# The last expert layer in 39 slots of 128 rows with copied input weights, and eight weight chunks split during the first routing

## The chip, the cores and the metric

One core of one Trainium2 chip. The metric is the device time of one execution in microseconds (us). The engines are TensorE (PE, its weight loads PEld), VectorE (DVE), ScalarE (ACT), GpSimd (POOL) and SyncE (SP, which only issues DMAs here). They run their own instruction streams and meet at semaphores.

## The reference

Two layers on x of 2 x 1024 tokens of width 256. Each adds an attention-like part and then a mixture of 8 experts of which each token uses 2. Only the expert parts matter here:

```python
x = x + _L0_xattn_ref(_layernorm(x), ctx, ...)      # attention to 77 context rows
x = x + _L0_ffn_ref(_layernorm(x), ...)             # experts 256 -> 256 -> 256
x = x + _L1_xattn_ref(_layernorm(x), ctx, ...)      # a linear map
x = x + _L1_ffn_ref(_layernorm(x), ...)             # experts 256 -> 1024 -> 256
# _L1_ffn_ref
probs = softmax(x @ router_w.T + router_b); top_p, top_e = top_k(probs, 2)
for e in range(8):
    y = y + gate_e[:, None] * (gelu(x @ w1[e].T + b1[e]) @ w2[e].T + b2[e])
```

## The kernel before

All matrix products that matter are done in three fp16 products: each fp32 operand is kept as a high part and a low part (the rest), and `three` (line 1204, whose `mm` is line 1202) adds high x high, high x low and low x high in PSUM.

**Order of the stages.** Attention over 16 tiles of 128 tokens; routing of the first expert layer (`route(0)`); its slots; a token stage that gathers the expert results, adds the linear map and normalizes; routing of the last expert layer (`route(1)`); its slots; the sum into the output.

**Routing.** `route` on DVE is a chain of some fifty small operations on 128 x 128 numbers (lines 979 to 1060), with two products on TensorE between and one multiplication on POOL (`number_tokens`, line 527). It sorts the 4096 (token, expert) pairs by expert, each expert padded up to whole slots, and ends with `index`, the token of each place, from which POOL gathers. ACT adds two exponentials, which DVE waits for behind `index`.

**Slots.** A slot is 256 rows (`A = 2` tiles of 128) of one expert. Their number is fixed at the worst case, `NSLOT = (2*T + E*(SW-1)) // SW` = 23, 5888 rows. For slot j: POOL gathers two tiles of normalized rows from DRAM (`gather_rows`, line 536, two slots ahead, three buffers); TensorE transposes them (`slot_tr`, line 1400); DVE copies the columns out of PSUM (`slot_cols`, line 1068); TensorE multiplies by the expert's input weights (`slot_up`); DVE scales and adds the bias (`slot_bias`, line 1081); ACT applies gelu and writes the high part (lines 737, 741); DVE writes the low part (`slot_lo`, line 1090); TensorE multiplies by the output weights (`slot_down`); DVE adds the output bias (`slot_out`, line 1099). In the first layer SP stores the result, in the last one POOL scatters it by token (`scatter_y`, line 578). In the last layer a slot has 48 up matmuls whose stationary operand is a weight tile and whose moving operand is 256 rows, and 48 down matmuls whose moving operand is 256 weight columns. The expert of a slot is read into a register, and weights and biases are addressed through it:

```python
last = three(ps[:, hc, :], m.wa[:, bass.ds(e + o, P)], m.wa[:, bass.ds(e + (per + o), P)],
             xT[:, dc, :], xT[:, DC + dc, :], dc == 0, dc == DC - 1)
```

**Weight chunks.** The expert weights come as 44 chunks, most of 128 x 1024 fp32 (512 KB). SP loads a chunk into a staging buffer (`stage`); ACT writes the high part (`split_hi`, line 608), and for the chunks whose low part POOL makes also scales the staged values (line 611); the low part is made by POOL (`split_lo`, line 452, even chunks) or by DVE (line 849, odd chunks). Chunks 4 to 19 are split during attention, 20 to 39 one per slot step of the first expert layer, and the last four (40 to 43, all by POOL) just before POOL's part of the second routing. Four staging buffers are in turn from chunk 22 to 37.

**Queues.** Each engine works strictly in the order of its code. In the first layer POOL's order is: gather of slot j+2, then the low part of chunk 20+j if it is even. SP's order is: chunk 24+j, then the store of slot j-4; the bias broadcast `b2_loaded0` (1 MB) goes out once `index` is there. In the last layer POOL's is: gather of slot j+2, scatter of slot j-3.

## Time and profile before

| | |
|---|---|
| median of 3 runs | 822.01 us (821.63 to 823.38) |
| profiled execution | 821.37 us, its span 819.5 us |
| TensorE busy | 610.7 us, 75% of the span |
| DVE busy | 544.0 us, 66% |
| ACT busy | 378.6 us, 46% |
| POOL busy | 434.1 us, 53% |
| TensorE clock granted, mean | 0.872 of full speed |
| DMA | 70.27 MB, 86 GB/s over the span |

The span is the time from the first to the last instruction of the profiled execution; the execution's own time is 1.9 us longer. Busy shares are means over stages that have different limits. Clock 1.00 is 2.4 GHz, 0.50 is 1.2 GHz.

### The profile page before, as it was taken

To read this page: it belongs to the slowest core of one execution; us is meant where nothing else is said; L and a number is where in the kernel's file an instruction comes from. 1 tells how busy PE (TensorE), PEld (TensorE's weight loads), DVE (VectorE), ACT (ScalarE), POOL (GpSimd) and SP (SyncE) were. 2 spreads that over 40 slices of the span, in tenths; PEclk is the share of its full clock that TensorE was granted. 3 is DMA by queue.
4 is the path that set the end of the run, shared out by engine and by line. 5 is a ranking of instruction groups with operands and counts; after the bars stand their busy time and mean duration, and the time that the engine had idled before them with its cause. 6 is when DMAs were issued, how large, how long until landed. Compare 5 with 4: busy or idle time off the path is not lost.

```text
span 819.5 us, 16876 instructions
## 1 busy us (share of the span) xinstructions
PE 610.7 (75%) x5984; PEld 539.1 (66%) x5984; DVE 544.0 (66%) x975; ACT 378.6 (46%) x568; POOL 434.1 (53%) x406
## 2 busy tenths in 40 slices
PE   5957889999996416779544553079999999999960
PEld 4646888889985315567432443068898889888850
DVE  3963689999988675668446776945555555555527
ACT  2644267777765315555314666324344443333420
POOL 6663668988886137767328863453333333332120
PEclk9986699999998757889985776579999999999995
DMA  8201002211222426776742322021111111111018
GB/s 277 78 3 28 26 2 66 66 50 50 66 66 65 118 72 180 220 217 166 219 137 82 98 78 79 5 78 42 50 46 48 53 53 54 48 47 39 21 38 303
DMA packets 35824, 70.27 MB, mean 86 GB/s; under 512 B 5985, under 2 KB 22114, under 8 KB 35490
## 3 DMA queue, kind: packets, MB, share of 16 engines
q1 hardware_dynamic: 25442, 42.70, 16.8%
q0 software_dynamic: 8160, 22.29, 9.8%
q10 hardware_dynamic: 2144, 4.19, 1.4%
q8 instruction: 54, 0.88, 0.5%
q14 instruction: 24, 0.20, 0.1%
HBM read 50.81 MB, written 18.35 MB: 84 GB/s over the span
## 4 chain that ended last, share of the span: by engine, by line
PE 48%; DVE 21%; issue 8%; POOL 8%; DMA 7%; ACT 7%; SPq 0%; POOLq 0%; ACTq 0%; DVEq 0%
PE banks L1202 45%; DMA slot_region<-normed_rows,index 4%; PE banks L1400 2%; POOL wb_region L568 2%; POOL slot_region L536 1%; DVE x_res L1129 1%; DVE w_region L895 1%; DVE rs L887 1%; DVE w_region L900 1%; ACT w_region L675 1%; POOL w_region L452 1%; DMA w_region<-token_y 1%; DVE w_region L1034 1%; DVE slot_region L1034 1%; POOL rv L476 1%
## 5 line engine op out<-in xcount | busy, mean ns | idle before, releaser
L1202 PE MATMUL banks<-w_region 128*128 128x128 f16 (+5 forms) x1948 | 174.9, 251 | 31.9 <-POOL w_region L527 12.1
L1202 PEld LDWEIGHTS banks<-w_region 128*128 128x128 f16 (+1 forms) x1948 | 160.7, 126 | 41.4 <-POOL w_region L527 12.4
L1202 PE MATMUL banks<-w_region,wb_region 128*128 (+1 forms) x1168 | 137.9, 277 | 11.8 <-DMA wb_region<-wk 6.6
L1202 PEld LDWEIGHTS banks<-w_region,wb_region 128*128 128x128 f16 (+1 forms) x1168 | 119.2, 105 | 26.0 <-issue 7.9
L578 POOL DMA_INDIRECT token_y<-slot_region,lg x46 | 45.4, 987 | 157.6 <-DVE slot_region L1099 150.6
L737 ACT ACTIVATE wb_region<-wb_region 128x1024 f32<-128x1024 f32 x46 | 48.6, 1057 | 166.7 <-DVE wb_region L1081 166.7
L1202 PE MATMUL banks<-slot_region,w_region 128*128 128x256 f16 x1104 | 125.3, 274 | 0.0
L1202 PEld LDWEIGHTS banks<-slot_region,w_region 128*128 x1104 | 107.6, 98 | 12.6
L536 POOL DMA_INDIRECT slot_region<-normed_rows,index x92 | 91.9, 999 | 36.2 <-issue 23.8
L1081 DVE SCALAR_TENSOR_TENSOR wb_region<-banks,b_s 128x1024 f32<-128x1024 f32 x46 | 56.2, 1224 | 70.0 <-PE banks L1202 70.0
L1090 DVE TENSOR_TENSOR wb_region<-wb_region 128x1024 f16<-128x1024 f32 x46 | 56.2, 1221 | 25.7 <-ACT wb_region L741 25.7
L1202 PE MATMUL banks<-wb_region,w_region 128*128 (+1 forms) x344 | 54.4, 309 | 16.0 <-ACT w_region L642 10.1
L1202 PEld LDWEIGHTS banks<-wb_region,w_region 128*128 128x128 f16 (+1 forms) x344 | 40.1, 122 | 27.9 <-ACT w_region L642 13.1
L1400 PE MATMUL banks<-ident_h,slot_region 128*128 128x128 f16 x368 | 31.3, 234 | 34.7 <-DMA slot_region<-normed_rows,index 34.5
L487 POOL TENSOR_TENSOR rq<-rq,neghalf 128x16 f32<-128x16 f32 x16 | 47.8, 2984 | 6.8 <-DVE rq L863 6.8
L1400 PEld LDWEIGHTS banks<-ident_h,slot_region 128*128 128x128 f16 x368 | 25.7, 104 | 38.6 <-DMA slot_region<-normed_rows,index 37.2
L741 ACT ACTIVATE wb_region<-wb_region 128x1024 f16<-128x1024 f32 x46 | 48.6, 1057 | 1.5
L1068 DVE COPY slot_region<-banks 128x1024 f16<-128x1024 f16 x46 | 31.4, 683 | 26.7 <-PE banks L1400 26.7
L499 POOL TENSOR_TENSOR w_region<-w_region,rs 128x1232 f32<-128x1232 f32 x16 | 36.0, 2249 | 18.5 <-DVE rs L890 18.4
L452 POOL TENSOR_TENSOR w_region<-staging,w_region 128x1024 f16<-128x1024 f32 x15 | 32.0, 2136 | 22.7 <-ACT staging L611 22.6
L1202 PE MATMUL banks<-slot_region,wb_region 128*128 128x256 f16 x276 | 40.4, 305 | 0.0
L687 ACT ACTIVATE w_region<-banks 128x512 f16<-128x512 f32 (+1 forms) x48 | 23.4, 522 | 36.4 <-PE banks L1313 36.4
(237 smaller groups left out, 1077.2 us busy)
## 6 DMA issues: line engine op xcount, KB each, us to landing
staging<-w_t SPq DMA_DIRECT2D x24, 512.0 KB, 4.2
sorted_y<-slot_region SPq DMA_DIRECT2D x23, 256.0 KB, 4.7
w_region<-w_t SPq DMA_DIRECT2D x8, 512.0 KB, 5.5
x_res<-x SPq DMA_DIRECT2D x4, 512.0 KB, 9.7
staging<-w_in SPq DMA_DIRECT2D x4, 512.0 KB, 3.7
normed_rows<-w_region SPq DMA_DIRECT2D x16, 128.0 KB, 1.7
staging<-w_out SPq DMA_DIRECT2D x4, 512.0 KB, 3.7
normed_rows<-wb_region SPq DMA_DIRECT2D x16, 128.0 KB, 2.0
```

The lines of the kernel that those rows point to most:

```text
L452: g.tensor_tensor(chunks[k][2], staged(k), chunks[k][1], ALU.subtract).then_inc(sem(f"chunk_lo{k % 2}"), 1)
L487: link(g.tensor_tensor(v, v, neghalf[:, 0:1].to_broadcast([P, NH]), ALU.pow))
L499: g.tensor_tensor(p_rows(i), p_rows(i), rs[:, :, None].to_broadcast([P, NH, L]), ALU.mult).then_inc(sem("weights_ready"), 1)
L536: g.indirect_dma_start(out=m.rows[:, j % RING, a, :], out_offset=None, in_=rows_dram, in_offset=bass.IndirectOffsetOnAxis(ap=index[:, q:q ...
L578: g.indirect_dma_start(out=y_token, out_offset=bass.IndirectOffsetOnAxis(ap=back[:, q:q + 1], axis=0), in_=moes[1].y[:, j % YB, a, :], in_ ...
L737: s_.activation(v, v, ACT.Gelu_apprx_tanh).then_inc(sem("gelu"), 1)
L741: s_.activation(m.hh[:, j % 2, a * m.HH:(a + 1) * m.HH, :], v, ACT.Copy).then_inc(sem(f"h_hi{layer}"), 1)
L1068: v.tensor_copy(m.xT[:, j % 2], slot_columns(j)).then_inc(sem(f"slot_cols{layer}"), 1)
L1081: v.scalar_tensor_tensor(out=m.g[:, u % 2], in0=hidden(m, u), scalar=1.0 / WS, in1=bias[:, :, None].to_broadcast([P, m.HH, SW]), op0=ALU.m ...
L1090: v.tensor_tensor(m.hl[:, j % 2, c, :], m.g[:, u % 2], m.hh[:, j % 2, c, :], ALU.subtract).then_inc(sem(f"h_lo{layer}"), 1)
L1202: return t.matmul(o, a, b, start=start, stop=stop)
L1400: last = t.transpose(cols[:, c, a * P:(a + 1) * P], m.rows[:, j % RING, a, c * P:(c + 1) * P], ident_h[:, :])
```

## The change

**Last layer.** Slots are 128 rows (`TILES = (2, 1)`), and there are 39 of them, 4992 rows. The first layer keeps 23 slots of 256. A slot has 4 transposes, 48 up matmuls with 128 moving columns and 24 down matmuls with 256. Gathers run four slots ahead in a ring of eight tiles; results have four buffers. Before each slot DVE copies the high and low input weights of its expert (8 KB a partition) into `w_slot`, which lies over the two staging buffers, in two halves of hidden units (`slot_weights`, each a COPY of 4 x 512 fp16 a partition). The copy of a half waits until TensorE has finished that half of the slot before (`half_up`), and the up matmuls wait for their half's copy and take their weights from the fixed place. Bias, gelu and low part work on the whole slot of 128 x 1024 at once. The last layer's `slot_down` trails `slot_up` by two slots and not by one.

**First routing.** Chunks 20 to 27 (`ROUTED`) are split between attention and slots: ACT makes both of its passes over each of them before `route(0)`'s exponentials, POOL makes all eight low parts before `number_tokens`. SP no longer waits for `index` with the bias broadcast, which goes out behind chunk 23, and then stages up to chunk 31.

**First layer's slots.** Twelve chunks (28 to 39) remain, one at every second slot step, six on POOL and six on DVE. The order of the chunks in memory is changed with that: both weights of experts 0 to 3 first, then those of 4 to 6, then those of 7.

Some semaphores are shared between the layers, with counts that run on.

```diff
-    A = 2
-    SW = A * P
-    NSLOT = (2 * T + E * (SW - 1)) // SW
-    NQ = A * NSLOT
+    TILES = (2, 1)
+    NSLOTS = [(2 * T + E * (a * P - 1)) // (a * P) for a in TILES]
+    NQS = [a * n for a, n in zip(TILES, NSLOTS)]
+    LAG = 2
...
-        chunks += [c for e, c in big if e < E - 1] + [c for e, c in big if e == E - 1]
+
+        for part in (range(E // 2), range(E // 2, E - 1), range(E - 1, E)):
+            chunks += [c for e, c in big if e in part]
...
+        R_CH = 8
         LATE = 2 * (per // CH)
+        ROUTED = range(PRE + A_CH, PRE + A_CH + R_CH)
+        WITH_SLOTS = range(ROUTED.stop, NCH - LATE)
+
+        def by_pool(k):
+            return k % 2 == 0 or k in ROUTED or k >= NCH - LATE
...
-            return k // 2 + 1 if k < NCH - LATE else (NCH - LATE) // 2 + k - (NCH - LATE) + 1
+            return sum(by_pool(n) for n in range(k + 1))
+
+        def chunk_of(s):
+            return WITH_SLOTS[s // 2] if s % 2 == 0 and s // 2 < len(WITH_SLOTS) else None
...
+            m.A, m.NSLOT, m.NQ = TILES[layer], NSLOTS[layer], NQS[layer]
+            m.SW = m.A * P
+            m.RING, m.AHEAD, m.YB = ((3, 2, 3), (8, 4, 4))[layer]
+            m.rows, at = carve(SLR, 0, [m.RING, m.A, 2 * D], F16)
+            m.xT, at = carve(SLR, at, [2, 2 * DC, m.SW], F16)
+            m.y, at = carve(SLR, at, [m.YB, m.A, D], F32)
...
+        w_slot = STG[:, :, :].rearrange("p a b -> p (a b)").bitcast(F16).rearrange("p (s n) -> p s n", n=H1)
...
             for k in RINGED[0:2]:
                 stage(k)
-            sp.wait_ge(sem("routed"), 1)
             load(moes[0].b2, b_out0.partition_broadcast(P), "b2_loaded0")
-            for j in range(NSLOT + 4):
-                if RINGED.start + 2 + j < RINGED.stop:
-                    stage(RINGED.start + 2 + j)
-                elif 0 <= j - len(RINGED) < 4:
-                    stage(RINGED.stop + j - len(RINGED))
+            for k in range(RINGED.start + 2, ROUTED.stop + 4):
+                stage(k)
+
+            stage_at = {k: 2 * (k - 4 - ROUTED.stop) for k in range(ROUTED.stop + 4, RINGED.stop)}
+            stage_at |= {k: 2 * (min(k, RINGED.stop + 1) - 2 - ROUTED.stop) for k in range(RINGED.stop, RINGED.stop + 2)}
+            stage_at[RINGED.stop] = stage_at[RINGED.stop + 1]
+            stage_at |= {k: 2 * (k - 2 - ROUTED.stop) for k in range(NCH - LATE, NCH - LATE + 2)}
+            for j in range(NSLOTS[0] + 4):
+                for k in sorted(stage_at):
+                    if stage_at[k] == j:
+                        stage(k)
                 if j >= 4:
-                    keep_y(0, j - 4)
+                    keep_y(j - 4)
...
             def split_lo(k):
 
                 pool.wait_ge(sem("chunk_scaled"), scaled(k))
+                if k % 2:
+                    pool.wait_ge(sem("chunk_lo1"), k // 2)
                 g.tensor_tensor(chunks[k][2], staged(k), chunks[k][1], ALU.subtract).then_inc(sem(f"chunk_lo{k % 2}"), 1)
...
+                for j in range(m.AHEAD):
                     gather_rows(layer, j)
                 if layer == 1:
                     pool.wait_ge(sem("back_ready"), 1)
-                for j in range(NSLOT + 3 * layer):
-                    if j + AHEAD < NSLOT:
-                        gather_rows(layer, j + AHEAD)
+                for j in range(m.NSLOT + 3 * layer):
+                    if j + m.AHEAD < m.NSLOT:
+                        gather_rows(layer, j + m.AHEAD)
                     if layer == 1 and j >= 3:
                         scatter_y(j - 3)
                     if layer == 0:
-                        k = PRE + A_CH + j
-                        if k < NCH - LATE and k % 2 == 0:
+                        k = chunk_of(j)
+                        if k is not None and by_pool(k):
                             split_lo(k)
...
+            for k in ROUTED:
+                split_lo(k)
             slot_rows(0)
...
+            act.wait_ge(sem("attn_done"), NT)
+            for k in ROUTED:
+                split_hi(k)
             route(0)
             act.wait_ge(sem("gates_ready"), 1)
-            for s in range(NSLOT + 1):
-                if s < NSLOT and PRE + A_CH + s < NCH - LATE:
-                    split_hi(PRE + A_CH + s)
+            for s in range(NSLOTS[0] + 1):
+                if chunk_of(s) is not None:
+                    split_hi(chunk_of(s))
                 if s >= 1:
                     gelu(0, s - 1)
...
+            def expert_at(j):
+                expert_of[j] = dve.value_load(expert[0:1, 0, j:j + 1], min_val=0, max_val=E - 1)
+
+            def slot_weights(j, a):
+
+                m = moes[1]
+                if j >= 1:
+                    dve.wait_ge(sem("half_up"), 2 * (j - 1) + a + 1)
+                half = slice(a * m.H // 2, (a + 1) * m.H // 2)
+                src = m.wa[:, bass.ds(expert_of[j] * (2 * DC * m.H), 2 * DC * m.H)].rearrange("p (s n) -> p s n", n=m.H)
+                v.tensor_copy(w_slot[:, :, half], src[:, :, half]).then_inc(sem("slot_weights"), 1)
+
+            def slot_bias(layer, j):
 
                 m = moes[layer]
-                u = m.PARTS * j + a
-                if a == 0:
-                    expert_of[j] = dve.value_load(expert[0:1, 0, j:j + 1], min_val=0, max_val=E - 1)
-                dve.wait_ge(sem(f"slot_h{layer}"), u + 1)
-                if u >= 2:
-                    dve.wait_ge(sem(f"h_lo{layer}"), u - 1)
-                bias = m.b[:, bass.ds(expert_of[j] * m.HC + a * m.HH, m.HH)]
-                v.scalar_tensor_tensor(out=m.g[:, u % 2], in0=hidden(m, u), scalar=1.0 / WS,
-                                       in1=bias[:, :, None].to_broadcast([P, m.HH, SW]),
-                                       op0=ALU.mult, op1=ALU.add).then_inc(sem(f"h_biased{layer}"), 1)
-
-            def slot_lo(layer, j, a):
+                dve.wait_ge(*up_done(layer, j + 1))
+                if j >= 2:
+                    dve.wait_ge(sem("h_lo"), made(layer, j - 1))
+                bias = m.b[:, bass.ds(expert_of[j] * m.HC, m.HC)]
+                v.scalar_tensor_tensor(out=m.g[:, j % 2], in0=hidden(m, j), scalar=1.0 / WS,
+                                       in1=bias[:, :, None].to_broadcast([P, m.HC, m.SW]),
+                                       op0=ALU.mult, op1=ALU.add).then_inc(sem("h_biased"), 1)
...
+            def slots_of_last():
+                dve.wait_ge(sem("b1_loaded"), 16)
+                dve.wait_ge(sem("b2_loaded1"), 16)
+                for b in range(2):
+                    dve.wait_ge(sem(f"chunk_lo{b}"), NCH // 2)
+                n = NSLOTS[1]
+                for s in range(-1, n + LAG + 1):
+                    if s + 1 < n:
+                        slot_cols(1, s + 1)
+                        expert_at(s + 1)
+                        for a in range(2):
+                            slot_weights(s + 1, a)
+                    if 0 <= s < n:
+                        slot_bias(1, s)
+                    if 0 <= s - LAG - 1 < n:
+                        slot_out(1, s - LAG - 1)
+                    if 0 <= s - 1 < n:
+                        slot_lo(1, s - 1)
...
+            def slot_up_last(j):
+
+                m = moes[1]
+                pe.wait_ge(sem("slot_cols"), made(1, j + 1))
+                if j >= 2:
+                    pe.wait_ge(sem("h_biased"), made(1, j - 1))
+                xT, ps = m.xT[:, j % 2], hidden(m, j)
+                for a in range(2):
+                    pe.wait_ge(sem("slot_weights"), 2 * j + a + 1)
+                    for hc in range(a * m.HC // 2, (a + 1) * m.HC // 2):
+                        w = slice(hc * P, (hc + 1) * P)
+                        for dc in range(DC):
+                            last = three(ps[:, hc, :], w_slot[:, dc, w], w_slot[:, DC + dc, w],
+                                         xT[:, dc, :], xT[:, DC + dc, :], dc == 0, dc == DC - 1)
+                    last.then_inc(sem("half_up"), 1)
```

## Rows read from the trace of the kernel before

**Rows 1.** Windows: start:end, length, busy us (x instructions) by engine, PEclk, DMA share, GB/s.
```profile
270.00:304.00 34.00, 9.17 (x109) 7.50 (x107) 25.92 (x64) 8.32 (x15) 8.38 (x6) 0.63 0.26 78
304.00:425.00 121.00, 83.81 (x736) 68.23 (x736) 71.36 (x105) 59.56 (x77) 69.82 (x58) 0.88 0.67 192
...
536.00:789.00 253.00, 250.06 (x2362) 224.21 (x2363) 139.52 (x137) 97.17 (x92) 85.08 (x87) 0.99 0.16 47
```

**Rows 2.** Timeline of one slot, last layer: start, duration, engine, line, operation [idle before].
```profile
611.50 0.61 PE L1400 MATMUL banks<-ident_h,slot_region 128*128 128x128 f16 x8
...
611.95 5.40 PE L1202 MATMUL banks<-slot_region,w_region 128*128 128x256 f16 x48
...
614.87 1.23 DVE L1081 SCALAR_TENSOR_TENSOR wb_region<-banks,b_s 128x1024 f32<-128x1024 f32 x1 [1.76 <-PE banks L1202]
...
617.19 5.40 PE L1202 MATMUL banks<-w_region,wb_region 128*128 x48
...
622.43 0.61 PE L1400 MATMUL banks<-ident_h,slot_region 128*128 128x128 f16 x8
```

**Rows 3.** Timeline of TensorE in the attention stage.
```profile
130.71 6.12 PE L1202 MATMUL banks<-w_region 128*128 128x128 f16 x78
136.67 1.04 PE L1313 MATMUL banks<-w_region 128*128 128x128 f32 x8
```

**Rows 4.** Groups by line and shape: count, busy us, mean ns, idle before.
```profile
L1202 PEld LDWEIGHTS banks<-slot_region,w_region 128*128 x1104 | 107.6, 98 | 12.6
...
L1090 DVE TENSOR_TENSOR wb_region<-wb_region 128x1024 f16<-128x1024 f32 x46 | 56.2, 1221 | 25.7 <-ACT wb_region L741 25.7
...
L1068 DVE COPY slot_region<-banks 128x1024 f16<-128x1024 f16 x46 | 31.4, 683 | 26.7 <-PE banks L1400 26.7
...
L905 DVE SCALAR_TENSOR_TENSOR x_res<-banks,x_res 128x256 f32<-128x256 f32 x16 | 6.7, 417 | 2.7 <-PE banks L1202 2.6
```

**Rows 5.** Timeline at both ends of the last expert layer.
```profile
532.25 1.07 POOL L536 DMA_INDIRECT slot_region<-normed_rows,index  x1 [4.15 <-DVE index L1049]
...
536.48 1.03 PE L1400 MATMUL banks<-ident_h,slot_region 128*128 128x128 f16 x8 [5.38 <-DMA slot_region<-normed_rows,index]
...
539.71 1.70 PE L1202 MATMUL banks<-slot_region,w_region 128*128 128x256 f16 x7
...
787.13 5.40 PE L1202 MATMUL banks<-w_region,wb_region 128*128 x48 [1.09 <-DVE slot_region L1099]
...
794.94 0.97 POOL L578 DMA_INDIRECT token_y<-slot_region,lg  x1 [0.30 <-issue]
```

**Rows 6.** Timeline: start of the first routing, and its first gather.
```profile
282.87 0.29 DVE L979 TENSOR_REDUCE w_region<-lg 128x16 f32<-128x128 f32 x1
...
304.22 1.23 POOL L536 DMA_INDIRECT slot_region<-normed_rows,index  x1 [4.17 <-DVE index L1049]
```

**Rows 7.** Timeline of the second routing, DVE and POOL.
```profile
505.30 4.25 POOL L452 TENSOR_TENSOR w_region<-staging,w_region 128x1024 f16<-128x1024 f32 x2 [5.05 <-ACT staging L611]
505.42 2.15 DVE L986 SCALAR_TENSOR_TENSOR slot_region<-slot_region,lg 128x128 f32<-128x128 f32 x1
...
507.92 1.77 DVE L981 TENSOR_TENSOR slot_region<-slot_region 128x128 f32<-128x128 f32 x1
509.73 0.29 DVE L982 TENSOR_TENSOR slot_region<-slot_region,first 128x128 f32<-128x128 f32 x1
...
513.34 2.12 POOL L452 TENSOR_TENSOR w_region<-staging,w_region 128x1024 f16<-128x1024 f32 x1 [3.80 <-ACT staging L611]
513.42 2.07 DVE L1001 TENSOR_TENSOR slot_region<-slot_region 128x8 f32<-128x8 f32 x1
```

**Rows 8.** Timeline: TensorE's slot transposes in the first expert layer.
```profile
309.60 1.04 PE L1400 MATMUL banks<-ident_h,slot_region 128*128 128x128 f16 x8 [6.55 <-DMA slot_region<-normed_rows,index]
...
357.63 0.61 PE L1400 MATMUL banks<-ident_h,slot_region 128*128 128x128 f16 x8
...
360.70 0.61 PE L1400 MATMUL banks<-ident_h,slot_region 128*128 128x128 f16 x8
...
409.73 0.61 PE L1400 MATMUL banks<-ident_h,slot_region 128*128 128x128 f16 x8
```

**Rows 9.** Waits, 304 to 425 us: total us, times, longest.
```profile
PE banks L1400 <- DMA slot_region<-normed_rows,index: 27.8, 8, 6.6
```

More of the change, by code:

```diff
@@ L85, in build @@
     VW_STEP = 4
-    AHEAD = 2
-    RING = 3
-    YB = 3
     with ExitStack() as ctx:
@@ L290, in build, with slot_columns, slot_banks, hidden @@
         LAST = slice(FULL * 6, NH)
-        def slot_columns(j):
-            return bank[7 * (j % 2)].bitcast(F16)[:, 0:2 * DC * SW].rearrange("p (c t) -> p c t", t=SW)
-        def slot_banks(j):
-            b = 5 if A == 2 else 5 + j % 2
-            return PSUM[:, b:b + A, 0:D]
-        def hidden(m, u):
-            b = 1 + 2 * (u % 2)
-            return PSUM[:, b:b + 2, :].rearrange("p b (c t) -> p (b c) t", t=SW)[:, 0:m.HH, :]
+        def slot_columns(m, j):
+            return bank[7 * (j % 2)].bitcast(F16)[:, 0:2 * DC * m.SW].rearrange("p (c t) -> p c t", t=m.SW)
+        def slot_banks(m, j):
+            b = 5 if m.A == 2 else 5 + j % 2
+            return PSUM[:, b:b + m.A, 0:D]
+        def hidden(m, j):
+            b = 1 + 2 * (j % 2)
+            return PSUM[:, b:b + 2, :].rearrange("p b (c t) -> p (b c) t", t=m.SW)[:, 0:m.HC, :]
+        def made(layer, n):
+            return layer * NSLOTS[0] + n
+        def up_done(layer, n):
+            return (sem("half_up"), 2 * n) if layer else (sem("slot_h"), n)
+        def gathered(layer, j):
+            k = j % moes[layer].RING
+            first = TILES[0] * len(range(k, NSLOTS[0], moes[0].RING)) if layer and k < moes[0].RING else 0
+            return sem(f"rows_gathered{k}"), 16 * (first + TILES[layer] * (j // moes[layer].RING + 1))
         block = ctx.enter_context(nc.Block())
@@ L531, in gather_rows @@
                 m = moes[layer]
-                for a in range(A):
-                    if j >= RING:
-                        pool.wait_ge(sem(f"slot_tr{layer}"), j - RING + 1)
-                    q = A * j + a
+                for a in range(m.A):
+                    if j >= m.RING:
+                        pool.wait_ge(sem("slot_tr"), made(layer, j - m.RING + 1))
+                    q = m.A * j + a
                     g.indirect_dma_start(
-                        out=m.rows[:, j % RING, a, :], out_offset=None, in_=rows_dram,
+                        out=m.rows[:, j % m.RING, a, :], out_offset=None, in_=rows_dram,
                         in_offset=bass.IndirectOffsetOnAxis(ap=index[:, q:q + 1], axis=0)).then_inc(
-                        sem(f"rows_gathered{layer}_{j % RING}"), 16)
+                        gathered(layer, j)[0], 16)
             def slot_rows(layer):
@@ L545, in slot_rows @@
                     pool.wait_ge(sem(f"rows_kept{1 + 2 * layer}_{b}"), 16 * (NT // 2))
-                for j in range(AHEAD):
+                m = moes[layer]
+                for j in range(m.AHEAD):
                     gather_rows(layer, j)
@@ L1393, in slot_tr @@
                 m = moes[layer]
-                pe.wait_ge(sem(f"rows_gathered{layer}_{j % RING}"), 16 * A * (j // RING + 1))
+                pe.wait_ge(*gathered(layer, j))
                 if j >= 2:
-                    pe.wait_ge(sem(f"slot_cols{layer}"), j - 1)
-                cols = slot_columns(j)
-                for a in range(A):
+                    pe.wait_ge(sem("slot_cols"), made(layer, j - 1))
+                cols = slot_columns(m, j)
+                for a in range(m.A):
                     for c in range(2 * DC):
-                        last = t.transpose(cols[:, c, a * P:(a + 1) * P], m.rows[:, j % RING, a, c * P:(c + 1) * P],
+                        last = t.transpose(cols[:, c, a * P:(a + 1) * P], m.rows[:, j % m.RING, a, c * P:(c + 1) * P],
```

228 lines of the change are left out of this document (110 added, 118 removed).

## The prediction

> **What bounds the kernel now.** I read the page first for its totals, then the busy times by stretch [rows 1]. They show stages with different limits, so the page's 75% busy TensorE says little. In the last expert layer (536 to 789 us) TensorE is busy 250.06 of 253 us at a granted clock of 0.99: nothing else matters there. In the first expert layer (304 to 425) it is busy 83.8 of 121 us, with the DMA engines at 0.67. Between and behind them lie the token stages and the second routing, which the change hardly touches.
>
> Next the timeline of one slot of the last layer [rows 2]. A slot of 256 rows takes 622.43 - 611.50 = 10.93 us. The 48 matmuls of `slot_up` take 617.19 - 611.95 = 5.24 us, 109.2 ns each at 256 columns; `slot_down` is as long; what is left for the 8 transposes is 0.45 us, 56 ns each. So 23 slots are 251 us of pure matmul stream, and the only way to shorten it is to stream fewer columns. For the price of 128 columns I looked for a stretch of the attention stage with such matmuls [rows 3]: 78 matmuls of the `q_proj` and `attn` loops (48 of 128 columns, 30 of 256) run from 130.71 to the next group at 136.67, 5.96 us. Less 30 x 109.2 = 3.28, 48 took 2.68 us, 56 ns each.
>
> **Last layer, the slot.** A slot of 128 rows has 4 transposes (0.22), 48 up matmuls of 128 columns (2.68) and 24 down matmuls of 256 columns (2.62): 5.52 us. 39 of them are 215.3 us, against 251.4. The saving is 4992 padded rows for 5888.
>
> It holds only if DVE keeps up, since it now copies each slot's input weights too: two COPYs of 128x2048 f16 within SBUF. No row has that shape. DVE's rows [rows 4] go from 417 ns at 256 fp32 elements to 1221 at 1024: 1.05 ns an element and 0.15 us fixed. The f16 COPY out of PSUM, 683 ns for 1024, is (683 - 150)/1024 = 0.52 ns an element. At that pace a copy is 0.15 + 1.07 = 1.22 us; the upper end is 0.15 + 2048 x 1.05 = 2.30 us, the lower end the fixed 0.15. I take 1.22, as COPY in f16 is the nearest row. A 512-element column copy is then 0.42, the output add of 256 elements 0.42.
>
> Now the order on DVE. Call T the end of the first half of up(s) on TensorE. DVE sees a finished half 0.30 us later (611.95 + 2.62 = 614.57; the bias starts at 614.87 [rows 2]), and I let following operations overlap by 0.08, as they do in a busy stretch. Copy one runs T+0.30 to 1.44. Copy two waits for the second half (T+1.34+0.30) and ends at 2.78, bias (1.22) at 3.92, output add at 4.26, low part (1.22) at 5.40, columns at 5.74. The next half is due at T+5.52+0.30 = 5.82. So DVE fits with 0.08 us to spare at 1.22 us a copy, and with about 0.6 at half that. Above 1.31 us a copy the slot becomes 2 x copy + 2.9. The read of the expert number in front of the copies I cost at nothing, as a wait stands behind it; without that cover 0.1 us would cost 39 x 0.1 = 4 us. ACT is busy 97 of 253 us with the same passes over 5888 rows [rows 1] and gets fewer; POOL has one gather and one scatter a slot at 0.97 + 0.30 = 1.27 each [rows 5]. Both are hidden under 5.5.
>
> **Last layer, its ends** [rows 5]. The first slot now needs one gather, not two. The first gather is issued at 532.25, and tr(0) now waits until 536.48 for the second one, 1.3 later. tr(0) can come at about 535.1; tr(1) waits for the next gather (536.5), then up(0) starts at about 537.0 and not 539.71: -2.7. The stream from there: 39 x (2.68 + 2.62) + 37 x 0.22 = 214.8, plus 2 for the half clock at its start and 0.4 for the first low part, 217.2. It was 252.7, from 539.71 to 787.13 + 48 x 0.109 = 792.4: -35.5. At the end one scatter of 1.27 and 0.27 of output add go. Together **-39.7 us**. The route arithmetic is as long as before: 39 for 46 columns of places, 273 for 161 expert comparisons, some tenths of either sign.
>
> **First routing.** Before, DVE starts it at 282.87 and the first gather goes out at 304.22 [rows 6], with POOL busy for 8.4 us and ACT for 8.3 of the 34 around it [rows 1]. Now ACT does two passes and POOL one subtraction for each of eight chunks in it, and SP sends the chunks and the bias broadcast (1 MB) earlier. What that costs can be read in the second routing, where POOL splits four late chunks [rows 7]: L986 takes 2.15 us and L981 1.77 while POOL's subtraction runs, against 0.29 for the like operation at 509.73, and L1001 takes 2.07. A DVE operation with two SBUF inputs waits for POOL's subtraction to end. The four stretch by 1.86, 1.48, 1.90 and 1.90: 1.79 on the mean. Eight subtractions, nearly back to back like the first two there (4.25 us for both), each catch one: 8 x 1.79 = **+14.3 us** of later first gather. Bounds: nothing, if all fell into DVE's waits; 8 x 2.13 = 17, and some us more if the chunks come late. POOL's own next work, `number_tokens`, waits for DVE anyway, and ACT's two exponentials are due later than its last chunk.
>
> **First expert layer.** The transposes of its 23 slots start at 309.60 and 409.73 at the ends [rows 8]: 4.55 us a slot. Undisturbed ones follow at 357.63 and 360.70, 3.07 us. The excess is 100.1 - 22 x 3.07 = 32.6 us, of which TensorE waited 27.8 us in 8 waits for gathered rows [rows 9]. These come late because POOL issues them behind a subtraction that waits for ACT and for a chunk, and because 0.5 MB chunks share the DMA engines. Now 12 chunks are split here, not 20, and they are loaded well ahead. If the excess falls with the chunks (12/20), 13 us go; POOL's own demand, 2 x 1.27 + 2.13 x 6/23 = 3.1 a slot, is as long as TensorE's 3.07, so not all 32.6 can go. I take between 13 and 21: **-17 us**. The first gathers also lose the 1 MB broadcast beside them: -1.
>
> **Sum.** -39.7 + 14.3 - 17 - 1 = -43.4. The profiled execution took 821.4 us (span 819.5 and 1.9 around it), which lies 0.6 under the median of 822.0. 821.4 - 43.4 = 778.0.
>
> **Rivals.**
> A, the routing is not stretched, since the chunks come late or fall into DVE's gaps: 778 - 14 = 764. For it: ACT must wait for chunks 22 to 24 through the DMA. Against: later subtractions only meet later DVE operations.
> B, the first layer keeps its pace, bound by the way issue to landing with a ring of three: 778 + 17 = 795. For it: the gathers' waits [rows 9]; against: 3.07 us stretches exist with all chunk work in them.
> C, the weight copies are slow, and DVE bounds the last layer. At one element per 1.05 ns a copy is 2.30, the slot 2 x 2.30 + 2.9 = 7.5: 39 x 2.0 = 78 more, 856 and slower than before. It decides from 1.31 us a copy, and eats the whole gain from 1.88 us. For it: no row has an SBUF copy of this size; against: the pace of the f16 COPY [rows 4].
> D, the weight loads no longer hide. A load lasts 98 ns [rows 4], longer than 56; were it the pace, 48 x 42 = 2.0 us a slot, 39 x 2.0 = 79, 857. Against it are the 48 matmuls of that stretch [rows 3], each with a load of its own. The Trainium skill (TensorE: Matmul & The Clock Gate, section Back-to-back issue gap) says that a stream of load and matmul pairs of 128 columns sustains about 81 ns each. By that figure the slot would grow by 1.2 us and the gain of the last layer would be gone; the 56 ns of this trace disagree.
>
> **How the numbers follow.** Forecast 0.63, A 0.12, B 0.13, C 0.06, D 0.03, others 0.03. The likeliest gives 778, its own range 768 to 789. 762 to 797 takes in A and B and leaves out about 0.15. A difference of 0.2% (1.6 us) is about what can be told from none here. Slower: C, D and a part of the others, 0.09; the same 0.01; faster 0.90.
>
> **What would show it.** Last layer: transposes 5.5 us apart, TensorE without a gap, DVE waiting shortly before each first copy, a COPY of 128x2048 at 1.2 us or less. Routing: two-input DVE operations of about 2 us beside POOL's L452, and the first gather some 35 us after the routing's start instead of 21. First layer: fewer waits for gathered rows, under 4 us a slot. I am wrong if the copy is over 1.3 us, or is itself held by POOL's gathers and scatters, which no row shows.

## The result, and the profile after

The changed kernel took 781.6 us (median of 4 runs, 778.7 to 784.9) where the kernel before took 822.1 us (821.6 to 823.4) beside it. The ratio is 0.9511, with a 95% interval of 0.9477 to 0.9545. The forecast was 778.0, with a range of 762 to 797. A second set of five runs beside eleven of the kernel before, on another chip, gave 782.1 us and a ratio of 0.9534 (0.9511 to 0.9557). The profiled execution of the changed kernel took 783.2 us, with a span of 781.4.

First the granted clock and the busy times by stretch, in the changed kernel: the first expert layer (317 to 426 us) and the last one (538 to 756). Columns as in [rows 1].

```profile
317.00:426.00 109.00, 81.33 (x736) 68.72 (x736) 66.87 (x102) 47.64 (x65) 58.65 (x53) 0.88 0.57 162
538.00:756.00 218.00, 217.39 (x2956) 205.91 (x2954) 166.68 (x231) 82.48 (x78) 107.08 (x73) 0.99 0.15 46
```

TensorE is still full in the last layer, 217.4 of 218 us, and the layer is now 38 us shorter. VectorE (DVE) has gone up there from 139.5 of 253 us [rows 1] to 166.7 of 218.

Next the timeline of one slot of the last layer, which answers to [rows 2].

```profile
639.89 0.39 PE L1464 MATMUL banks<-ident_h,slot_region 128*128 128x128 f16 x4
...
640.12 2.84 PE L1265 MATMUL banks<-slot_region,staging 128*128 128x128 f16 x48
...
641.77 0.69 DVE L1119 COPY staging<-w_region 128x2048 f16 x1 [0.56 <-PE banks L1265]
642.04 1.26 POOL L570 DMA_INDIRECT slot_region<-normed_rows,index  x1 [0.30 <-issue]
...
642.80 2.78 PE L1265 MATMUL banks<-w_region,wb_region 128*128 x24
643.11 0.70 DVE L1119 COPY staging<-w_region 128x2048 f16 x1 [0.65 <-PE banks L1265]
643.73 1.21 DVE L1128 SCALAR_TENSOR_TENSOR wb_region<-banks,b_s 128x1024 f32<-128x1024 f32 x1
644.86 0.41 DVE L1143 SCALAR_TENSOR_TENSOR slot_region<-banks,wb_region 128x256 f32<-128x256 f32 x1
...
645.19 1.21 DVE L1135 TENSOR_TENSOR wb_region<-wb_region 128x1024 f16<-128x1024 f32 x1
...
645.42 0.39 PE L1464 MATMUL banks<-ident_h,slot_region 128*128 128x128 f16 x4
```

The slot takes 645.42 - 639.89 = 5.53 us, forecast 5.52. The 48 up matmuls go from 640.12 to the down products at 642.80, 2.68 us, 56 ns each, as priced from [rows 3]. DVE's order is the one of the prediction, and it waits 0.56 and 0.65 us before the two copies. Each copy takes 0.70 us, not 1.22.

Then the first routing, where the second group answers to [rows 6] and the first to what was expected from [rows 7]: DVE and POOL, timeline.

```profile
283.08 0.29 DVE L1018 TENSOR_REDUCE w_region<-lg 128x16 f32<-128x128 f32 x1
...
284.58 2.12 POOL L485 TENSOR_TENSOR w_region<-staging,w_region 128x1024 f16<-128x1024 f32 x1 [5.15 <-ACT staging L647]
284.70 2.15 DVE L1025 SCALAR_TENSOR_TENSOR w_region<-w_region,lg 128x128 f32<-128x128 f32 x1
...
291.33 4.30 POOL L485 TENSOR_TENSOR w_region<-w_region 128x1024 f16<-128x1024 f32 x2
291.79 1.79 DVE L1039 COPY w_region<-w_region 128x7 f32<-128x7 f32 x1
293.62 2.04 DVE L1040 TENSOR_TENSOR w_region<-w_region 128x8 f32<-128x8 f32 x1
...
317.44 1.24 POOL L570 DMA_INDIRECT slot_region<-normed_rows,index  x1 [4.17 <-DVE index L1088]
```

From the routing's start to the first gather it is now 34.36 us; it was 21.35. Each of POOL's eight subtractions holds one DVE operation until it ends: a copy of 7 elements lasts 1.79 us, and 0.17 in the kernel before. The eight held operations together last 13.0 us longer than the same operations in the kernel before, which is the whole delay.

Last, the slot transposes of the first layer and TensorE's waits for gathered rows in it, which answer to [rows 8, 9].

```profile
321.75 1.03 PE L1464 MATMUL banks<-ident_h,slot_region 128*128 128x128 f16 x8 [5.47 <-DMA slot_region<-normed_rows,index]
...
410.11 0.61 PE L1464 MATMUL banks<-ident_h,slot_region 128*128 128x128 f16 x8
```

```profile
PE banks L1464 <- DMA slot_region<-normed_rows,index: 21.5, 8, 5.5
```

22 steps take 88.4 us, 4.02 us a slot; it was 4.55 [rows 8]. The waits went only from 27.8 to 21.5 us, still eight of them. The first of them (6.6 us before, 5.5 now) stands ahead of the first transposes and so outside these 22 steps.

The two profiled executions differ by 819.5 - 781.4 = 38.1 us, which splits at four landmarks (after minus before). Start of routing to first gather: +13.0. First gather to the end of the first layer (POOL's iota, which waits for the last kept rows, 425.84 against 424.14): -11.5. From there to the first gather of the last layer (532.31 against 532.25): -1.6. From that gather to the last scatter: -38.1. What lies ahead of the routing and behind the last scatter makes up the rest, +0.1.

### The profile page after: what moved, and what is told of

The parts are those of the page before. It is cut to its first block, busy times and chain, and to the rows that moved or that the text cites. A ratio compares the mean times of both kernels' runs of the same rounds, so it can differ in the third digit from the quotient of the medians.

```text
span 781.4 us, 17877 instructions
## 1 busy us (share of the span) xinstructions
PE 574.4 (74%) x6556; PEld 520.0 (67%) x6556; DVE 578.9 (74%) x1067; ACT 368.2 (47%) x558; POOL 461.5 (59%) x396
## 4 chain that ended last, share of the span: by engine, by line
PE 46%; DVE 25%; issue 8%; ACT 7%; POOL 7%; DMA 6%; SPq 0%; DVEq 0%; ACTq 0%; POOLq 0%
PE banks L1265 43%; DMA slot_region<-normed_rows,index 4%; PE banks L1464 2%; POOL wb_region L603 2%; DVE x_res L1191 1%; DVE w_region L933 1%; DVE heads L925 1%; DVE w_region L938 1%; ACT w_region L711 1%; POOL slot_region L570 1%; DMA w_region<-token_y 1%; DVE w_region L1073 1%; DVE slot_region L1073 1%; DVE w_region L861 1%; ACT w_region L687 1%
## 5 line engine op out<-in xcount | busy, mean ns | idle before, releaser
L1265 PE MATMUL banks<-w_region,wb_region 128*128 (+1 forms) x1000 | 122.2, 278 | 11.3 <-DMA wb_region<-wk 6.9
L612 POOL DMA_INDIRECT token_y<-slot_region,lg x39 | 65.6, 1682 | 101.5 <-DVE slot_region L1143 101.2
L1265 PEld LDWEIGHTS banks<-w_region,wb_region 128*128 128x128 f16 (+1 forms) x1000 | 101.4, 107 | 22.8 <-issue 8.0
L1265 PE MATMUL banks<-slot_region,staging 128*128 128x128 f16 x1872 | 112.9, 221 | 0.7 <-DVE staging L1119 0.7
L1265 PEld LDWEIGHTS banks<-slot_region,staging 128*128 128x128 f16 x1872 | 108.1, 99 | 1.0 <-issue 0.9
L1119 DVE COPY staging<-w_region 128x2048 f16 x78 | 54.4, 700 | 46.2 <-PE banks L1265 45.7
L520 POOL TENSOR_TENSOR heads<-heads,neghalf 128x16 f32<-128x16 f32 x16 | 47.7, 2982 | 6.8 <-DVE heads L901 6.8
L1128 DVE SCALAR_TENSOR_TENSOR wb_region<-banks,b_s 128x1024 f32<-128x1024 f32 x39 | 47.1, 1207 | 2.0 <-PE banks L1265 2.0
L532 POOL TENSOR_TENSOR w_region<-w_region,heads 128x1232 f32<-128x1232 f32 x16 | 36.0, 2248 | 18.5 <-DVE heads L928 18.4
L1107 DVE COPY slot_region<-banks 128x512 f16<-128x512 f16 (+1 forms) x62 | 31.7, 511 | 14.7 <-PE banks L1464 14.6
```

What stands on the lines that cost most here:

```text
L520: link(g.tensor_tensor(v, v, neghalf[:, 0:1].to_broadcast([P, NH]), ALU.pow))
L532: g.tensor_tensor(p_rows(i), p_rows(i), rs[:, :, None].to_broadcast([P, NH, L]), ALU.mult).then_inc(sem("weights_ready"), 1)
L612: g.indirect_dma_start(out=y_token, out_offset=bass.IndirectOffsetOnAxis(ap=back[:, j:j + 1], axis=0), in_=m.y[:, j % m.YB, 0, :], in_offs ...
L1119: v.tensor_copy(w_slot[:, :, half], src[:, :, half]).then_inc(sem("slot_weights"), 1)
L1128: v.scalar_tensor_tensor(out=m.g[:, j % 2], in0=hidden(m, j), scalar=1.0 / WS, in1=bias[:, :, None].to_broadcast([P, m.HC, m.SW]), op0=ALU ...
L1265: return t.matmul(o, a, b, start=start, stop=stop)
```

## The experiments

The 12 kernels ran in three groups of four; each was timed beside the kernel before on its own chip, so ratios are compared, not times. The kernel before stood at 826.9, 819.9 and 819.4 us in the three.

### The two parts alone

The last layer alone: the changed kernel, with

```
-        R_CH = 8
+        R_CH = 0
-            return WITH_SLOTS[s // 2] if s % 2 == 0 and s // 2 < len(WITH_SLOTS) else None
+            return WITH_SLOTS[s] if s < len(WITH_SLOTS) else None
```

and SyncE's order of loads as in the kernel before. The new order of the chunks in memory stays.

> The last layer as after the change, the weight chunks split where the kernel before splits them (none in the first routing, one with each slot of the first layer). Theory: the whole gain is the last layer's (the traces give it 38.1 us of 38.1), and the chunk part is worth nothing: 13.2 us of later first gather against 12.6 us from the first slots. That gives 783 to 785. Rival, the prediction's own sum (the chunk part is worth -3.7 us): 785 to 787, with the changed kernel at 781.6. Rival two, the chunk part costs something, since its first gathers are later: 778 or less.

Measured: ratio 0.9494 (0.9462 to 0.9526), on the 822 us of the first set 780.5. That is under the 783 to 785 expected, and its interval (777.9 to 783.1) leaves out the 785 to 787 of the prediction's sum. The last layer alone gives as much as both parts, as far as these intervals can tell.

The chunks alone: the kernel before with

```
+        R_CH = 8
+            for k in ROUTED:
+                split_lo(k)
             slot_rows(0)
...
+            act.wait_ge(sem("attn_done"), NT)
+            for k in ROUTED:
+                split_hi(k)
             route(0)
```

and `chunk_of`, `by_pool`, SyncE's order and the order of the chunks in memory of the changed kernel.

> The kernel before, with the changed kernel's schedule of weight chunks and nothing else. Theory: about 822 as before, within 2 us, as 13.2 us of later first gather are given back by 12.6 us in the first layer. The prediction's sum for this part, +14.3 - 17 - 1 = -3.7, gives 818. Rival: it is slower, 825 or more, since only the last layer gained.

Measured: 1.0142 (1.011 to 1.0173), some 834 us on the 822 of the first set. That is far from the expectation and from the prediction's sum, and on the side of the rival (825 or more). The profile showed gaps of TensorE inside a row of matmuls that depend on nothing new. Timeline of that kernel:

```profile
385.15 0.38 PE L1227 MATMUL banks<-slot_region,wb_region 128*128 128x256 f16 x2 [0.29 <-issue]
...
386.57 0.27 PE L1227 MATMUL banks<-slot_region,wb_region 128*128 128x256 f16 x1 [1.04 <-issue]
```

"issue" means that the profile knows nothing that the engine waited for. The same kernel was timed again in another group:

> The kernel before with the changed chunk schedule, timed again. In its first profile TensorE had 8.4 us of gaps in the first layer that no engine and no transfer released, and the part measured +1.4%, where the changed kernel against the last layer alone makes the same part +0.3 to +0.4%. Theory: those gaps belong to the program's place in memory or to the chip of that call and are no property of the schedule: without them it stands within 0.5% of the kernel before. Rival: they come again, and it is 1.2 to 1.6% slower.

Measured: 0.9995 (0.997 to 1.0021), and the waits of the two profiles in the first layer (305 to 435 us), the first run above and the second below:

```profile
PE banks L1425 <- DMA slot_region<-normed_rows,index: 9.5, 3, 5.5
PE banks L1227 <- DVE slot_region L1124: 9.0, 7, 2.4
PE banks L1425 <- issue: 8.4, 4, 3.2
```

```profile
PE banks L1425 <- DMA slot_region<-normed_rows,index: 20.2, 9, 5.5
...
PE banks L1227 <- DVE slot_region L1124: 3.4, 3, 1.5
```

So one and the same program was 1.4% slower on one chip and unchanged on another, and the gaps without a releaser were there only on the first. The schedule alone does not make them. What does stays open. Three of the four kernels of that group had 7 to 11 us of such gaps in the first layer (not the last layer alone, 0.6), so the times of these three say little; below they are called the disturbed group. In the second measurement the chunk part is worth nothing: 0.9995, and the forecast of -3.7 us (0.9955) lies just outside the interval.

### What stretches the first routing

```
+                if k in ROUTED:
+                    lo, raw_v, hi = lo[:, 0:8], raw_v[:, 0:8], hi[:, 0:8]
```

in POOL's `split_lo`: it subtracts 8 of 1024 columns and leaves the other low parts out.

> The changed kernel, but POOL's subtraction of the eight chunks of the first routing is done on 8 of their 1024 columns only (the low parts of these weights are left out otherwise). Transfers and ACT's passes stay. Theory: the 13.2 us are DVE operations held by POOL's subtraction, so the time from the routing's start to the first gather falls from 34.4 to about 21.5 us and the kernel to about 769. Rival: the chunks' transfers or ACT's passes set the gap, which then stays at 30 us or more, and the time at 779 or more.

Measured: ratio 0.9556 (0.9519 to 0.9594), in the disturbed group. The routing is read from the trace; timeline of POOL and the routing's first DVE operation:

```profile
284.03 0.29 DVE L1021 TENSOR_REDUCE w_region<-lg 128x16 f32<-128x128 f32 x1
...
303.65 0.20 POOL L488 TENSOR_TENSOR w_region<-w_region 128x8 f16<-128x8 f32 x1 [1.83 <-ACT w_region L650]
303.81 2.66 POOL L564 TENSOR_TENSOR w_region<-w_region,tokens 128x1472 f16<-128x1472 f16 x1
309.01 1.24 POOL L573 DMA_INDIRECT slot_region<-normed_rows,index  x1 [2.54 <-DVE index L1091]
```

The routing takes 309.01 - 284.03 = 24.98 us: 9.4 of the 13.0 us are gone, and the small DVE operations that took about 2 us (L1039 and L1040 above among them) are back under 0.45. DVE's own chain shows it whole: from its first operation to the last one ahead of its wait it takes 17.9 us, 33.4 in the changed kernel and 20.4 in the kernel before. So the stretch is POOL's subtraction. The other 3.6 us are a second limit under the first: ACT's sixteen passes end at 303.6, the last small subtraction waits for them, and POOL's `number_tokens` (L564) stands behind it. DVE was then the one that waited, 6.1 us. The expectation of 21.5 missed that. The kernel's time came nowhere near the 769 expected: behind the shorter routing its first layer lasted 120.3 us instead of 108.4, with 9.0 us of gaps without a releaser and 12.4 us of waits for DVE in it.

Four chunks instead of eight in the routing, the others spread over the slots, beside the changed kernel again:

```
-        R_CH = 8
+        R_CH = 4
+            return next((k for k in WITH_SLOTS if slot_of(k) == s), None)
```

> The changed kernel with four weight chunks split in the first routing instead of eight, and the other four back with the slots. Theory: each chunk in the routing costs 13.2 / 8 = 1.65 us and gives about as much back in the slots, so this is within 3 us of the changed kernel. The prediction's reading (DVE operations stretched one for one) puts the first gather 27.8 us after the routing's start. Rival: there is an optimum between none and eight, as the first four chunks fall into DVE's waits for free, and this is 4 us or more faster than both.

> The changed kernel itself, timed again beside the next ones on one chip, since its runs spread over 6 us. Expected within 1% of its first ratio of 0.951 to the kernel before. Theory: the last layer alone measured 0.9494, so the chunk part is worth between nothing and a small loss, and this comes out at 0.949 to 0.953. Rival: the chunk part is a gain here too and this ends under 0.947.

Measured: 0.9496 (0.9463 to 0.9529) for four chunks, and 0.9534 (0.9511 to 0.9557) for the changed kernel. The first gather of the former, by its timeline:

```profile
282.12 0.29 DVE L1020 TENSOR_REDUCE w_region<-lg 128x16 f32<-128x128 f32 x1
...
309.93 1.24 POOL L572 DMA_INDIRECT slot_region<-normed_rows,index  x1 [4.17 <-DVE index L1090]
```

27.81 us, as expected. The four-chunk kernel is 3.1 us faster than the changed kernel beside it, with intervals that overlap a little, and level with the last layer alone (0.9494, on another chip). So the expectation (within 3 us) held about, and the rival (4 us or more faster than both) did not come. The changed kernel itself came out just above the 0.949 to 0.953 expected of it. Over the undisturbed profiles the routing and the first layer trade like this (start of routing to first gather, plus first gather to the layer's end):

| chunks in the routing | profiles | routing | first layer | sum |
|---|---|---|---|---|
| none | before, last layer alone, and the same with late chunks on DVE | 21.3 | 119.9, 118.9, 116.5 | 141.3, 140.2, 137.8 |
| four | this one, and the same with late chunks on DVE | 27.8, 27.7 | 109.2, 109.4 | 137.0, 137.0 |
| eight | changed kernel twice, chunks alone again, late chunks on DVE, and the two kernels below that change only the last layer | 34.4, 34.9, 34.9, 35.1, 34.5, 34.8 | 108.4, 106.7, 104.5, 104.8, 107.9, 106.9 | 142.8, 141.6, 139.4, 139.8, 142.4, 141.7 |

Each chunk in the routing costs 1.6 to 1.7 us. By the means of these rows the first four give back about 9 us together, the next four about 3. Profiles with the same first layer differ by up to 4 us, so the 3 is not far from that spread; that the first layer comes to a floor is likely, not shown.

### What the first layer still waits for

The changed kernel with only the first 8 of 1024 columns of each chunk loaded during the slots (the splits keep their size, at scale 1 for these chunks):

```
+                if k >= ROUTED.stop + 4:
+                    sp.dma_start(dst[:, 0:8], src[:, 0:8]).then_inc(loaded, 16)
+                    return
```

> The changed kernel, but the chunks that are loaded during the first layer's slots bring only 8 of their 1024 columns (the rest of these weights is left out); all splits stay at their sizes. Theory: TensorE's 21.5 us of waits for gathered rows in the first layer come from sharing the DMA engines with ten 512 KB loads; the waits fall under 8 us and the first layer is 10 to 14 us shorter, about 769. Rival: the gathers are late since they are issued late on POOL, behind its subtractions, or by their own transfer time and the rows kept; the waits stay near 20 us, 781.

Measured: 0.9606 (0.957 to 0.9642), in the disturbed group. TensorE's waits in the first layer:

```profile
PE banks L1468 <- DMA slot_region<-normed_rows,index: 11.7, 5, 5.5
PE banks L1269 <- DVE slot_region L1147: 11.6, 8, 3.1
PE banks L1269 <- issue: 7.0, 7, 3.6
```

The waits for gathered rows fell from 21.5 to 11.7, but 18.6 us of others stand in their place, and the layer is no shorter (117.9 us from first gather to its end). As the chunks-alone kernel had 9.5 in its disturbed run and 20.2 in its other one, the fall says nothing of the loads. This one is inconclusive.

The traces of the two kernels do show where the waits stand. POOL gathers the rows of slot j+3 right behind the subtraction of step j. In the kernel before, POOL subtracts at every second step, and six of the eight waits (19.6 us) are for slots gathered right behind a subtraction. In the changed kernel it subtracts at every fourth, and all five slots gathered right behind one wait, 9.5 us together. One of them by timeline, POOL and TensorE:

```profile
338.81 2.22 POOL L485 TENSOR_TENSOR w_region<-w_region 128x1024 f16<-128x1024 f32 x1 [1.35 <-ACT w_region L647]
341.18 0.96 POOL L570 DMA_INDIRECT slot_region<-normed_rows,index  x1
...
348.08 1.03 PE L1464 MATMUL banks<-ident_h,slot_region 128*128 128x128 f16 x8 [2.87 <-DMA slot_region<-normed_rows,index]
```

The other three waits are for the first two slots (8.1 us, 8.2 before) and one of 4.0 us for the slot gathered at 395.99 and 397.24, beside which two chunks are loaded. So the part that stood behind subtractions did halve; the first two slots' waits stayed, and one came new. This is read from the places of the waits; no run moved the subtractions alone.

### What the last layer rests on

Without the copies: the up products read the weight region at an address from a register.

```
-                            last = three(ps[:, hc, :], w_slot[:, dc, w], w_slot[:, DC + dc, w],
+                            last = three(ps[:, hc, :], m.wa[:, bass.ds(e + o, P)], m.wa[:, bass.ds(e + (per + o), P)],
```

> The changed kernel without the copies of the input weights: the up products take their weights straight from the weight region, at addresses made from the slot's expert number in TensorE's registers. Theory: TensorE's queue pays for each address that is made from a register; with 128 rows a matmul lasts 56 ns, too short to cover it, so the slot grows from 5.52 us to 6.5 or more and the time to 820 or more. Rival, the copies buy nothing: the slot stays at 5.5 us, DVE is 1.4 us a slot less busy, and the time is the changed kernel's, 0.952 of the kernel before.

Measured: 844.8 us, ratio 1.0274 (1.0223 to 1.0325). Its slot, by the timeline:

```profile
641.13 4.10 PEld L1263 LDWEIGHTS banks<-slot_region,w_region 128*128 x48
...
641.14 4.23 PE L1263 MATMUL banks<-slot_region,w_region 128*128 128x128 f16 x48
...
645.36 2.53 PEld L1263 LDWEIGHTS banks<-w_region,wb_region 128*128 128x128 f16 x24
...
648.28 4.31 PE L1263 MATMUL banks<-slot_region,w_region 128*128 128x128 f16 x48
```

The slot is 648.28 - 641.14 = 7.14 us. The up products come one in (645.36 - 641.13) / 48 = 88 ns instead of 56, with no other engine to wait for. 39 x (7.14 - 5.53) = 63 us, about the difference to the changed kernel (1.0274 - 0.9534, times 822 = 61; from first gather to last scatter 59). The edit changes two things at once, how the address is made and the region that is read. The region is not what costs: the matmuls of [rows 3] have their operands in `w_region` too and take 56 ns. At 256 rows a matmul lasts 109 ns [rows 2] and covers the 88; at 128 it does not. Narrower slots without the copies made the kernel slower than before.

Each weight half copied twice:

```
+                cols = slice(half.start, half.start + 512)
+                dve.wait_ge(sem("extra_copies"), max(2 * j + a - 1, 0))
+                v.tensor_copy(scratch[:, a, :, 0:512], src[:, :, cols]).then_inc(sem("extra_copies"), 1)
```

> The changed kernel with each half of a slot's input weights copied twice (the first copy goes to memory that nobody reads): 1.40 us a half in place of 0.70, so just over the 1.31 us that the prediction gave as DVE's limit. By the prediction's 2 x copy + 2.9 the slot becomes 5.7 us and the kernel 0.18 x 39 = 7 us longer, 789. Rival one, DVE's operations don't overlap: 2.80 + 1.21 + 1.21 + 0.41 + 0.41 = 6.04 us a slot, 20 us longer, 802. Rival two, there is more slack than the prediction saw: the slot stays at 5.52 and the time at 782.

Measured: 785.9 us, ratio 0.9569 (0.9522 to 0.9616). Its interval overlaps that of the changed kernel (0.9534), so the slot decides. The slot, by the timeline:

```profile
642.80 0.39 PE L1468 MATMUL banks<-ident_h,slot_region 128*128 128x128 f16 x4
...
644.67 0.69 DVE L1122 COPY wb_region<-w_region 128x2048 f16 x1
645.28 0.70 DVE L1123 COPY staging<-w_region 128x2048 f16 x1
...
646.01 0.69 DVE L1122 COPY wb_region<-w_region 128x2048 f16 x1
646.62 0.70 DVE L1123 COPY staging<-w_region 128x2048 f16 x1
647.24 1.20 DVE L1132 SCALAR_TENSOR_TENSOR wb_region<-banks,b_s 128x1024 f32<-128x1024 f32 x1
...
648.32 0.39 PE L1468 MATMUL banks<-ident_h,slot_region 128*128 128x128 f16 x4
```

The slot stays at 648.32 - 642.80 = 5.52 us with DVE busy 69.6 of 70 us (640 to 710). Busy durations add to 6.0 us a slot, but in such a stretch each operation starts some 0.08 us before the one ahead has ended (644.67 + 0.69 = 645.36, next start 645.28). A pair of copies is so 1.32 us, not 1.40, and 2 x 1.32 + 2.9 = 5.54. So the 7 us expected did not come, since the expectation forgot the overlap inside the pair, and rival one falls; the slot of rival two (5.52) is what was measured. The prediction's model of DVE's order fits to 0.02 us, but as TensorE is busy all the time here (70.0 of 70 us), it is confirmed from one side only: no run has a copy long enough for DVE to set the slot.

### The second routing, and the best version

The low parts of the four last chunks made by DVE inside the second routing, not by POOL:

```
                 v.tensor_tensor(m2, m2, m1, ALU.subtract).then_inc(sem("route_shift"), 1)
+                if layer == 1:
+                    split_lo(NCH - LATE)
+                    split_lo(NCH - LATE + 1)
```

and the other two ahead of the wait for `tokens_done`.

> The changed kernel, but the low parts of the four last weight chunks are made by DVE inside the second routing (two after the routing's shift, two while it waits for POOL's token numbers) and not by POOL. Theory: POOL's four subtractions hold DVE operations of the second routing for about 6 us in all, and DVE needs 1.22 us for each chunk, of which two lie in a wait; the time from the second routing's start to the first gather, 27.9 us, falls by about 3.4 us, and the kernel to 778. Rival: DVE's own four passes take as much as they free: no change.

Measured: 0.9491 (0.9458 to 0.9524), profiled span 772.3 us. The routing starts at 498.60, and, by its timeline:

```profile
502.78 2.35 DVE L885 SCALAR_TENSOR_TENSOR w_region<-staging,w_region 128x1024 f16<-128x1024 f32 x2
...
519.86 2.36 DVE L885 SCALAR_TENSOR_TENSOR w_region<-staging,w_region 128x1024 f16<-128x1024 f32 x2
...
523.06 1.07 POOL L570 DMA_INDIRECT slot_region<-normed_rows,index  x1 [6.65 <-DVE index L1092]
```

24.46 us to the first gather against 27.87 in the changed kernel: -3.4, as expected. The rival falls. The intervals of the two ratios overlap a little; the trace carries this point.

With no chunk in the first routing, and with four; the same edit on these two kernels:

```
-        R_CH = 8
+        R_CH = 0
```

> Both parts that looked best: the last layer as after the change, the chunks of the first layer as before it, and the four last chunks' low parts made by DVE in the second routing. Theory: the last layer alone stood at 0.9494 of the kernel before, and the routing gives another 3.4 us (0.4%): 0.945. Rival: 0.949, if DVE's passes take what they free.

> Four chunks in the first routing instead of eight (0.9496 of the kernel before), and the four last chunks' low parts made by DVE in the second routing (worth 0.4%). Theory: the two add up, 0.945 to 0.946, the same as with no chunk in the first routing (0.9456). Rival: 0.9496, if what the second routing gives back depends on where the first layer ends.

Measured: 0.9456 (0.9426 to 0.9487) with none, 0.9446 (0.9407 to 0.9484) with four. Both add up as expected and can't be told from each other; the former, timed beside the changed kernel, beats it clearly (0.9534, intervals apart).

## Why the prediction came out right, step by step

- **Slot of the last layer**: 5.52 forecast, 5.53 measured. The narrower matmuls keep 56 ns. Rival D fell. The Trainium skill's figure (TensorE: Matmul & The Clock Gate, section Back-to-back issue gap) of some 81 ns for a load and matmul pair of 128 columns was not met here: 2.68 us / 48 = 56 ns with fixed addresses. Pairs with register addresses took 88.
- **Weight copies**: the mechanism right, the price too high, 0.70 for 1.22 us. The nearest row was a COPY out of PSUM; within SBUF an element takes half the time, (0.70 - 0.15) / 2048 = 0.27 ns. Rival C fell. The Trainium skill (VectorE: DVE Perf Modes, section The perf-mode tier table) gives 693 ns for a bf16 copy of 2048 elements within SBUF, and the trace agrees, with 0.70 us in fp16; the prediction had not drawn on it. The price did not matter, as even doubled copies fit.
- **Ends of the last layer**: -39.7 forecast for the whole, -38.1 measured. The up products start at 537.79 and not 537.0, since the first slot's first copy now stands before them: DVE starts it at 536.74, and it takes 0.75 us. The prediction had left it out of this place. The stream ran 218.3 us (to 756.08) for 217.2, the end gave 1.7 for 1.5.
- **First routing**: +14.3 forecast, +13.0 measured, and by the mechanism named: the kernel with small subtractions loses 9.4 of the 13.0 us, down to where ACT's passes end. Rival A fell. That only operations with two SBUF inputs wait was too narrow: a COPY of 7 elements waited too.
- **First layer**: the mis-sized term. Forecast -17 (13 to 21) and -1 for its first gathers; measured -11.8 between the transposes, -1.1 at the first gathers and +1.3 at its end. The rule "if the excess falls with the chunks" gave 13, and 11.8 came. What failed is the step from 13 to 17, for which the prediction had no row, and the end of the layer, put at nothing. The prediction also counted all 27.8 us of waits into an excess of 32.6 us that starts at the first transposes; 6.6 of them lie ahead of these. Nor is the fall even: the first four chunks taken out of the slots bring about 9 us, the second four about 3. Five slots gathered behind a subtraction, the first two slots and one more still wait; whether it is the place behind the subtraction that makes the five wait, no run tested. Rival B, that nothing of this term comes, fell too: 11.5 of 18 us came.
- **Sum**: the three errors are +1.6 (last layer), -1.3 (routing), and +6.5 (18 forecast, 11.5 come) in the first layer, less 1.6 that the stages between gave, which the sum had at nothing: +5.2, 783.2 of the profiled execution against 778.0. The median run was 781.6, 3.6 over the forecast. The mechanisms of the last layer and of the routing are those of the prediction; that the sum came this close is in part luck, as two errors took 2.9 us off the other two's 8.1, and no run explains the 1.6 between the stages.

The chunk part as a whole was forecast at -3.7 us and is worth 0 (0.9995 alone), so this part of the change was not worth making. The gain is the last layer's.

## What to carry to other kernels

When slots get narrower, ask what each instruction was covering: here a weight load at a register address costs 88 ns, free under a 109 ns matmul and 61 us in all above a 56 ns one, and a copy on an engine with room buys it off. Work moved into an idle engine is paid where it holds operations of a busy one: eight POOL subtractions of 2.1 us each cost DVE's chain 1.6 to 1.7 us apiece, while the gain on the other side is about 9 us for the first four and about 3 for the next. Sweep such a count, do not take an end of it.

## What the hardware showed beyond expectation

- A gather's issue on POOL took 1.23 us on the mean in the last layer, 0.98 before; in the slot shown it starts at 642.04 inside DVE's COPY of 641.77 to 642.46. Without the copies it was 0.97. A scatter's took 1.70 against 0.99, with and without the copies alike (1.71 without), so the copies are not its cause; in both it starts while DVE's low part of two SBUF inputs runs. In the changed kernel the last two scatters (754.31 and 756.93), with no such operation beside them, take 0.97. No run changes this alone. Both stay hidden.
- The same program ran at 1.4% over the kernel before on one chip and equal to it on another, with 10.8 us of unexplained gaps of TensorE ("issue") in the first layer on the first chip.
- With DVE busy 99% of the time, operations that follow each other without a wait overlap by some 0.08 us: their durations add to 6.0 us in a 5.52 us slot.
- The holding goes both ways. `number_tokens` on POOL takes 4.64 us in the changed kernel, beside two of DVE's f16 operations with 2048 elements, which take 6.95 us together. In the kernel with small subtractions DVE has done these two before, in 4.49 us, and `number_tokens` takes 2.66. So 2.0 of the 9.4 us gained there come from this.
